# Second layer's cross attention: the negated row maxima as three bf16 parts, added to the scores by a bf16 product

## The chip, the cores and the metric

The kernel runs on one core of one Trainium2 chip. The metric is the device time of one execution, in microseconds, as the median of several runs. The engines named below are PE (TensorE, matmuls; PEld are its weight loads), DVE (VectorE), ACT (ScalarE), POOL (GpSimd) and SP (SyncE, which only starts transfers here).

## The reference

A decoder of two layers on `x`, 16 batch elements of 128 tokens with 128 features, with a context of 77 rows for each batch element. Each layer is attention, cross attention to the context and a feed forward part, each added to its input and normalised. The first layer's feed forward is a mixture of experts. What the change touches is the second layer's cross attention, with 16 heads of 8 features:

```python
q = (einsum('bse,fe->bsf', query, wq) + bq).reshape(B, Sq, H, D).transpose(0, 2, 1, 3)
k = (einsum('bse,fe->bsf', key, wk) + bk).reshape(B, Sk, H, D).transpose(0, 2, 1, 3)
v = (einsum('bse,fe->bsf', value, wv) + bv).reshape(B, Sk, H, D).transpose(0, 2, 1, 3)
scores = einsum('bhqd,bhkd->bhqk', q, k) * scale
attn = softmax(scores, axis=-1)          # over the 77 context rows
out = einsum('bhqk,bhkd->bhqd', attn, v) # then the output projection
```

The softmax subtracts the maximum over the 77 keys for each query and head before the exponential. It is this subtraction that is done in another way.

## The kernel before

The work has three stages. In the first (to about 400 us) the first layer's attention and cross attention run over the 16 batch elements. In the second the experts run. The third, from about 458 us, holds the whole second layer, and the change belongs to it.

The third stage is software pipelined. `ORDER2` is a table that gives each engine the order of its steps within one round; the number behind a colon shifts a step by so many batch elements. In one round the decay attention (steps `d_...`) works on the next batch element, the cross attention (`e_...`) on the present one, and the feed forward part (`f_...`) on both sides of it. Each engine runs its list in order, and semaphores make it wait for the others. A step that waits holds all that stands behind it on its engine.

The cross attention of one batch element, with 16 heads as 4 strips of 32 partitions (index `i`) times 4 (index `a`):

- `e_s` (PE): scores with queries on the partitions, four banks of 4 x 77 columns.
- `e_m0` to `e_m3` (DVE, `row_max`, L1347): the negated maxima of a bank, 4 columns of the tile `nmb`.
- `e_nm` (PE, L942; ACT, L1095): `nmb` is turned by a transpose against the fp32 identity `ident` and copied to `nmT`, so that heads lie on partitions.
- `e_st` (PE, the rows `bank<-qa,k`): the scores again, now with keys on the partitions, 16 products that are left open.
- `e_inj` (PE, `less_max`, the rows `bank<-nmT,k_sb`): 16 products of a selecting table `picksel` with `nmT` add the negated maxima to the open scores. Each takes one strip of 32 partitions.
- `e_e0` to `e_e3` (ACT, L1105): the exponentials, then `e_v` (PE) with values and sums.

Around them on PE stand `f_up` (the convolution as products, `bank<-k,xdT`) ahead of `e_nm`; then `d_s01` (the first decay scores, `bank<-kbd`, weights `kbd`), `e_st`, `d_s3`, `e_inj` and `d_v` (`bank<-k,va`). On DVE `e_m3` is followed by `d_k` (L1657, which makes the keys that `d_s01` multiplies and which waits for POOL's `d_fade`), then `d_m0` and `d_m1` (the causal masks, L1663), `f_clamp` (L1755), `d_m2`, `d_m3` and `f_silu` (L1728). `d_s01` waits for `d_k`, `d_m0` for `d_s01`, `d_s3` for `d_m0`, `d_v` for `d_m3`. On ACT the order is `e_nm`, `f_exp`, `f_sig` (two passes, L1210 and L1211), then `e_e0`.

In the expert stage DVE runs, between relus of the experts' hidden rows (`m_hid`, L1578) and copies (`m_y`), `bias_parts`: it already splits the convolution's bias into three bf16 parts (L1612 to L1615).

Of the kernel before, what the change touches and what calls it, by code (L numbers as in the profile page):

```python
# [14 lines left out]
P = 128  # L15
B = 16
# [35 lines left out]
def offsets(sizes):  # L52
    at, found = 0, {}
    for name, n in sizes.items():
# [93 lines left out]
            "d_gate:2 d_q:2 e_m0:1 e_m1:1 e_m2:1 e_m3:1 d_k:2 d_m0:2 d_m1:2").split(),  # L148
    "act": ("e_e2 d_v:1 e_e3 c_ln:2 d_ln:1 e_v d_x:2 d_ln2:1 f_turn:-1 e_ln e_x:1 d_gates:2 e_q:1 f_ln:-1 f_x "
# [28 lines left out]
def decoder(nc, x_in, xT_in, cT_in, w_a, w_k, w_b, w_l, w_f, w_up, w_down, columns, rows, conv, consts, out,  # L178
            rel_dram, xg_dram, yg_dram):
    with ExitStack() as ctx:  # L180
        def sb(name, shape, dt=F32):
            return ctx.enter_context(nc.sbuf_tensor(name, shape, dt))
# [42 lines left out]
        ident = const("ident")  # L225
        picksel = const("picksel").rearrange("p (a j) -> p a j", a=4)

# [18 lines left out]
        nmxb, sumb, recb = sb("nmxb", [P, H]), sb("sumb", [P, H]), sb("recb", [P, H])  # L246
        nmb = sb("nmb", [P, P])
        nmT = sb("nmT", [P, P])
        rba = sb("rba", [P, P])
# [66 lines left out]
        ve, vd = va[0:2], va[2]  # L316
        nme, nmTe = nmb, nmT
        xE, xD = x1[0:2], [pTa[:, 6 + i, :] for i in range(2)]
# [138 lines left out]
        def _(pool):  # L457
# [3 lines left out]
            for t in va:  # L461
                G.memset(t[:], 0.0).then_inc(pre_pool, 1)
            G.memset(nmb[:], 0.0).then_inc(pre_pool, 1)
            G.memset(cum[:, 0, :], 0.0).then_inc(pre_pool, 1)
# [93 lines left out]
        def _(pe):  # L558
# [151 lines left out]
            def less_max(ps, ready):  # L710

                for a in range(4):
                    for i in range(4):
                        last = mm(ps[i][0:C, a * P:(a + 1) * P], picksel[strip(i), a, :], nmT[strip(i), :],
                                  start=False, stop=(a == 3))
                        if a == 3:
                            last.then_inc(ready, 1)
# [222 lines left out]
            def e_nm(t):  # L940
                pe.wait_ge(maxed["b"], 4 * (B + t) + 4)
                pe.transpose(bank[6][:, 3 * P:4 * P], nme[:], ident).then_inc(nm_ps, 1)  # L942

# [296 lines left out]
        def _(dve):  # L1240
# [103 lines left out]
            def row_max(i, b, base=0):  # L1344
                def f(t):
                    dve.wait_ge(scores["b"], 4 * (base + t) + i + 1)
                    V.tensor_reduce(nmb[:, 32 * i:32 * i + 4], bank[b][:, 0:4 * C].rearrange("p (a j) -> p a j", a=4),  # L1347
                                    AX.X, ALU.max, negate=True).then_inc(maxed["b"], 1)
                return f

            def b_max(i):
# [255 lines left out]
            def bias_parts():  # L1607

                dve.wait_ge(ld_conv, 32)
                step(V.tensor_scalar(cbias, cbias, const("third", 0, 1)[0:32, :], None, ALU.mult))  # L1610
                for i in (1, 2):
                    step(V.tensor_copy(cpart, cbias))  # L1612
                    step(V.scalar_tensor_tensor(out=cbias, in0=cpart, scalar=const("third", i, i + 1)[0:32, :], in1=cbias,
                                                op0=ALU.mult, op1=ALU.add))
                V.tensor_copy(cbrow[0:32, :], cbias).then_inc(w_ready, 1)  # L1615

# [147 lines left out]
            for n in range(1, 2 * E, 2):  # L1764
# [23 lines left out]
                **{f"d_m{i}": d_mask(i) for i in range(4)}, "d_add": d_out, "d_n0": d_n0, "d_n1": d_n1, "d_norm": d_norm,  # L1788
                **{f"e_m{i}": row_max(i, 3 + i, B) for i in range(4)}, "e_div": divide("e", 3, rbe, oTe), "e_add": e_out,
                "e_norm": norm("e", lambda t: xE[t % 2][:], normed["e"]), "v1": v1,  # L1790
# [5 lines left out]
def tables():  # L1796
    p, t = np.arange(P)[:, None], np.arange(P)[None, :]
    h2 = DH // 2
    freq = (1.0 / 10000.0 ** (np.arange(h2, dtype=np.float32) / np.float32(h2))).astype(np.float32)
    angle = (np.arange(P, dtype=np.float32)[None, :] * freq[(np.arange(P) % DH) // 2][:, None]).astype(np.float32)  # L1800
    sign = np.where(p % 2 == 0, -1.0, 1.0)
    n = np.arange(E + 1)
    row = np.arange(2 * B)
    band = np.arange(160)
    parts = {
        "ident": p == t,
        "tri": p < t,
        "causal": p <= t,
        "cos": np.cos(angle), "sin": np.sin(angle) * sign,
        "time": np.broadcast_to(t - MID, (P, P)),  # L1810
        "head16": (p // R) % 2 == np.arange(2),
        "rev": np.broadcast_to(E + 1 - n, (P, E + 1)),
        "cap": np.broadcast_to(np.where(n < E, CAP, 0), (P, E + 1)),
        "base": np.broadcast_to(n * P, (P, E + 1)),
        "trash": SLOTS + row[None, :] * P + p,
        "picksel": np.repeat(p % 32 == np.arange(4), C, axis=1),
        "onesband": np.broadcast_to(band % 40 < DH, (P, 160)),
        "third": np.concatenate([p < 3, -1 * (p >= 1), -1 * (p == 2)], axis=1),
    }
    return np.concatenate([np.asarray(parts[k], np.float32) for k in CONSTS], axis=1)  # L1820
# [81 lines left out]
```

## Time and profile before

| | |
|---|---|
| median of 3 runs | 760.44 us (759.88 to 760.55) |
| the profiled execution | 758.19 us |
| its span in the profile | 756.4 us |
| PE busy | 675.0 us, 89% of the span |
| DVE busy | 551.8 us, 73% |
| ACT busy | 404.5 us, 53% |
| POOL busy | 207.3 us, 27% |

The span is what the profiler sees from the first to the last instruction; the execution's own time is 1.8 us longer. Busy shares are means over three stages with different limits. An fp32 product appears as two records of a matmul, a bf16 product or a transpose as one. A weight load (PEld) can run while an earlier product is still under way.

### The profile page before, as it was taken

To read this page: it belongs to the slowest core of one execution; us is meant where nothing else is said; L and a number is where in the kernel's file an instruction comes from. 1 tells how busy PE (TensorE), PEld (TensorE's weight loads), DVE (VectorE), ACT (ScalarE), POOL (GpSimd) and SP (SyncE) were. 2 spreads that over 40 slices of the span, in tenths; PEclk is the share of its full clock that TensorE was granted. 3 is DMA by queue.
4 is the path that set the end of the run, shared out by engine and by line. 5 is a ranking of instruction groups with operands and counts; after the bars stand their busy time and mean duration, and the time that the engine had idled before them with its cause. 6 is when DMAs were issued, how large, how long until landed. Compare 5 with 4: busy or idle time off the path is not lost.

```text
span 756.4 us, 21349 instructions
## 1 busy us (share of the span) xinstructions
PE 675.0 (89%) x8334; PEld 519.1 (69%) x8334; DVE 551.8 (73%) x2013; ACT 404.5 (53%) x1172; POOL 207.3 (27%) x213
## 2 busy tenths in 40 slices
PE   5888999999999999999878988899899989999886
PEld 2445777777777787777766976666666666666664
DVE  1236778888888888987647557888888788888853
ACT  3756666666766666663210224555555555555542
POOL 5312233333333315423344112222222222222100
PEclk9969999999999999999879999999999999999999
DMA  9776435555444455630032110000000011111000
GB/s 345 271 257 205 162 130 172 171 171 170 166 160 124 123 172 178 231 147 20 20 103 69 33 32 9 10 11 13 13 16 13 13 14 14 15 13 13 5 6 7
DMA packets 48259, 72.22 MB, mean 95 GB/s; under 512 B 2832, under 2 KB 43280, under 8 KB 45472
## 3 DMA queue, kind: packets, MB, share of 16 engines
q1 hardware_dynamic: 45120, 61.80, 24.3%
q0 software_dynamic: 2320, 5.18, 3.3%
q10 hardware_dynamic: 720, 3.88, 1.3%
q8 instruction: 67, 1.10, 0.6%
q14 instruction: 32, 0.26, 0.1%
HBM read 32.38 MB, written 38.47 MB: 94 GB/s over the span
## 4 chain that ended last, share of the span: by engine, by line
PE 58%; DVE 22%; issue 8%; ACT 7%; DMA 2%; another core or an unknown queue 1%; POOL 1%; SPq 0%; DVEq 0%; ACTq 0%
PE bank L560 49%; PE bank L621 4%; PE bank L706 3%; DVE k L1663 3%; DVE scol L1705 2%; ACT kbd L1210 1%; ACT kbd L1211 1%; DMA xT_ld<-xT 1%; DVE k L1641 1%; DVE kbd L1755 1%; DVE q L1732 1%; DVE y_d L1679 1%; ACT pTb L1105 1%; DVE stats_e L1313 1%
## 5 line engine op out<-in xcount | busy, mean ns | idle before, releaser
L1066 ACT ACTIVATE sc<-sc,nmxa 128x128 f32<-128x128 f32 x256 | 79.9, 393 | 34.9 <-DVE nmxa L1290 34.9
L499 POOL TENSOR_TENSOR early<-early,recb 128x616 f32<-128x616 f32 x32 | 38.9, 1216 | 187.6 <-DVE recb L1378 187.6
L1290 DVE CUSTOM_DVE_ANT_0 sc<-bank,rel 128x128 f32<-128x128 f32 x256 | 56.4, 286 | 14.7 <-PE bank L560 14.5
L1663 DVE TENSOR_TENSOR k<-bank,k_sb 128x512 f32<-128x512 f32 x64 | 41.2, 685 | 28.6 <-PE bank L560 23.7
L1300 DVE COPY pTa<-bank 128x512 f32<-128x512 f32 x32 | 22.0, 690 | 32.7 <-PE bank L621 32.7
L1046 ACT ACTIVATE rext<-bank 128x512 f32<-128x512 f32 x64 | 34.8, 609 | 18.2 <-PE bank L560 18.2
L476 POOL TENSOR_TENSOR rext<-rext,ones 128x1008 f32<-128x1008 f32 x16 | 29.9, 1868 | 52.7 <-ACT rext L1046 52.7
L560 PE MATMUL bank<-k,xdT 128*128 128x512 f32 x96 | 43.8, 592 | 0.0
L535 POOL TENSOR_TENSOR oTb<-x_all,row_sb 128x128 f32<-128x128 f32 x16 | 7.3, 457 | 132.9 <-DVE pTa L1684 132.9
L1113 ACT ACTIVATE early<-early 128x308 f32<-128x308 f32 x64 | 27.4, 454 | 29.4 <-DVE early L1363 29.4
L621 PE MATMUL bank<-k_sb,sc 128*128 128x128 f32 x256 | 36.4, 288 | 7.3 <-issue 6.5
L560 PE MATMUL bank<-pTb,v 77*32 77x128 f32 x1024 | 34.5, 282 | 4.4 <-issue 2.2
L560 PEld LDWEIGHTS bank<-xTb,wb 128*128 128x128 f32 x256 | 29.8, 191 | 12.6 <-issue 12.6
L621 PEld LDWEIGHTS bank<-k_sb,sc 128*128 128x128 f32 x256 | 30.2, 148 | 11.9 <-issue 11.0
L508 POOL DMA_INDIRECT xg_dram<-x_all,to_slot x32 | 31.4, 980 | 24.8 <-DVE to_slot L1514 16.8
L525 POOL DMA_INDIRECT pTa<-yg_dram,of_slot x32 | 31.3, 980 | 23.3 <-DMA yg_dram<-sc 16.3
L1354 DVE TENSOR_REDUCE nmxb<-bank 128x4 f32<-128x308 f32 x64 | 28.8, 472 | 11.6 <-PE bank L560 8.1
L560 PE MATMUL bank<-kbd 32*128 32x256 f32 x256 | 36.2, 400 | 0.1
L560 PE MATMUL bank<-k_sb,ones 128*128 128x256 f32 x144 | 36.2, 401 | 0.0
L1105 ACT ACTIVATE pTb<-bank 77x512 f32<-77x512 f32 x64 | 34.2, 588 | 3.4 <-PE bank L560 3.4
L560 PE MATMUL bank<-wb,oTb 128*128 128x128 f32 x256 | 34.6, 292 | 1.0 <-issue 0.6
L706 PE MATMUL bank<-k_sb,early 128*77 128x128 f32 x256 | 33.4, 274 | 0.8 <-ACT xTb L1095 0.5
(275 smaller groups left out, 1839.3 us busy)
## 6 DMA issues: line engine op xcount, KB each, us to landing
rel_dram<-rext SPq DMA_DIRECT2D x16, 2040.0 KB, 7.3
rel<-rel_dram SPq DMA_DIRECT2D x16, 960.0 KB
rext<-w_up SPq DMA_DIRECT2D x1, 1792.0 KB, 9.4
rel<-w_down SPq DMA_DIRECT2D x1, 1792.0 KB, 7.7
wb<-w_b ACTq DMA_DIRECT2D x1, 1604.0 KB, 16.5
xT_ld<-xT SPq DMA_DIRECT2D x16, 64.0 KB, 7.3
x_all<-x ACTq DMA_DIRECT2D x1, 1024.0 KB, 11.8
rel<-rel_dram SPq DMA_DIRECT2D x16, 64.0 KB
```

The costliest lines, as they stand in the source:

```text
L476: G.tensor_tensor(rext[:, :, 0:MAX_REL - 1], rext[:, :, MAX_REL - 1:MAX_REL].broadcast_to(shape), ones[:, 0:1].unsqueeze(2).broadcast_to(s ...
L499: G.tensor_tensor(pB[:, part, :], pB[:, part, :], recb[:, part].unsqueeze(2).broadcast_to([P, 8, C]), ALU.mult).then_inc(b_even, 1)
L508: G.indirect_dma_start(out=xg_dram, out_offset=bass.IndirectOffsetOnAxis(ap=to_slot[:, 2 * t + k:2 * t + k + 1], axis=0), in_=x_all[:, t, ...
L525: G.indirect_dma_start(out=g[k][t % 3], out_offset=None, in_=yg_dram if t else yg_dram[0:(E + 1) * P], in_offset=bass.IndirectOffsetOnAxis ...
L560: return pe.matmul(out_, lhsT, rhs, start=start, stop=stop)
L621: last = pe.transpose(bank[i][:, a * P:(a + 1) * P], sc[:, 4 * i + a, :], ident)
L706: last = pe.transpose(bank[(6, 7, 4, 5)[i]][0:C, a * P:(a + 1) * P], pB[:, 4 * i + a, :], ident)
L1046: A.activation(rext[:, 4 * i:4 * i + 4, MAX_REL - 1:MAX_REL - 1 + P], bank[i][:].rearrange("p (a r) -> p a r", a=4), ACT.Copy).then_inc(r_ ...
L1066: last = A.activation(sc[:, h, :], sc[:, h, :], ACT.Exp, bias=nmxa[:, h:h + 1], scale=-1.0)
L1105: A.activation(dst[0:C, 4 * i:4 * i + 4, :], bank[b][0:C, :].rearrange("p (a i) -> p a i", a=4), ACT.Exp).then_inc(exped["b"], 1)
L1290: last = V.tensor_tensor_reduce(out=sc[:, h, :], in0=bank[i][:, a * P:(a + 1) * P], in1=rel[:, t % 2, h, :], scale=-1.0, scalar=FAR, op0=A ...
L1663: V.tensor_tensor(scd[:, 4 * i:4 * i + 4, :], bank[(1, 2, 0, 1)[i]][:].rearrange("p (a t) -> p a t", a=4), const("causal").unsqueeze(1).br ...
```

## The change

The four maxima of a strip no longer go straight into the tile that is turned, but into a small dense tile `nmx` (128 x 16, fp32). A new DVE step `e_sp` (`e_split`) behind `e_m3` splits them into three bf16 numbers that add up to the fp32 one: the value rounded to bf16, the remainder rounded to bf16, and what is then left. The three parts stand in 12 columns of each strip of `nme`, now a bf16 tile. `e_nm` turns it by an ordinary product with a bf16 identity, ACT copies it to the bf16 tile `nmTe`, and the injection multiplies it by a bf16 table in which each head picks all three of its parts. The two bf16 tables are cast once on DVE, in `bias_parts`. PE now waits for one count of `e_sp` in place of four of the maxima.

```diff
-            "d_gate:2 d_q:2 e_m0:1 e_m1:1 e_m2:1 e_m3:1 d_k:2 d_m0:2 d_m1:2").split(),
+            "d_gate:2 d_q:2 e_m0:1 e_m1:1 e_m2:1 e_m3:1 e_sp:1 d_k:2 d_m0:2 d_m1:2").split(),
...
-        nmb = sb("nmb", [P, P])
-        nmT = sb("nmT", [P, P])
+        nmx = sb("nmx", [P, 16])
+        nmr = sb("nmr", [P, 16])
+        nme = sb("nme", [P, P], BF16)
+        nmTe = sb("nmTe", [P, P], BF16)
+        identb = sb("identb", [P, P], BF16)
+        pickb = sb("pickb", [P, 4 * C], BF16)
...
-                        last = mm(ps[i][0:C, a * P:(a + 1) * P], picksel[strip(i), a, :], nmT[strip(i), :],
+                        last = mm(ps[i][0:C, a * P:(a + 1) * P], pickb[strip(i), a * C:(a + 1) * C], nmTe[strip(i), :],
                                   start=False, stop=(a == 3))
...
             def e_nm(t):
-                pe.wait_ge(maxed["b"], 4 * (B + t) + 4)
-                pe.transpose(bank[6][:, 3 * P:4 * P], nme[:], ident).then_inc(nm_ps, 1)
+                pe.wait_ge(maxed["b"], 4 * B + t + 1)
+                mm(bank[6][:, 3 * P:4 * P], nme[:], identb[:]).then_inc(nm_ps, 1)
...
-                    V.tensor_reduce(nmb[:, 32 * i:32 * i + 4], bank[b][:, 0:4 * C].rearrange("p (a j) -> p a j", a=4),
-                                    AX.X, ALU.max, negate=True).then_inc(maxed["b"], 1)
-                return f
+                    keep(f"e_m{i}", t, V.tensor_reduce(
+                        nmx[:, 4 * i:4 * i + 4], bank[b][:, 0:4 * C].rearrange("p (a j) -> p a j", a=4),
+                        AX.X, ALU.max, negate=True))
+                return f
+
+            def e_split(t):
+                by_strip = nmx[:].rearrange("p (i a) -> p i a", a=4)
+                left = nmr[:].rearrange("p (i a) -> p i a", a=4)
+                parts = [nme[:].rearrange("p (i x) -> p i x", x=32)[:, :, 4 * k:4 * k + 4] for k in range(3)]
+                after(max(done[f"e_m{i}", t] for i in range(4)))
+                need(dve, nm_ps, t)
+                step(V.tensor_copy(parts[0], by_strip))
+                V.tensor_tensor(left, by_strip, parts[0], ALU.subtract)
+                step(V.tensor_tensor(parts[1], by_strip, parts[0], ALU.subtract))
+                V.tensor_tensor(parts[2], left, parts[1], ALU.subtract).then_inc(maxed["b"], 1)
...
+                step(V.tensor_copy(identb[:], ident))
+                step(V.tensor_copy(pickb[:], const("picksel")))
                 V.tensor_copy(cbrow[0:32, :], cbias).then_inc(w_ready, 1)
...
-        "picksel": np.repeat(p % 32 == np.arange(4), C, axis=1),
+        "picksel": np.repeat((p % 32 < 12) & (p % 4 == np.arange(4)), C, axis=1),
```

`step(...)` makes DVE wait until the instruction has completed; an instruction without it lets the next one start behind it.

DVE's order in a round of the third stage, before. `out_sb` belongs to `f_norm`, the first `kbd` to `d_q`, `nmb` to the maxima, the second `kbd` to `d_k`, `k<-bank` to the masks.

```order
L1332 TENSOR_SCALAR out_sb<-y_f,mv_f,rstd_f 128x128 [waits f_inv,st_out0]
L1751 TENSOR_SCALAR k<-k 128x256 [waits d_gate0]
L1651 TENSOR_TENSOR kbd<-bank,early 128x512 [waits d_rank]
L1347 TENSOR_REDUCE nmb<-bank 128x4 [waits b_scores] x4
L1657 TENSOR_TENSOR kbd<-bank,k 128x256 [waits d_faded,d_rank]
L1663 TENSOR_TENSOR k<-bank,k_sb 128x512 [waits d_att] x2
```

The same place after:

```order
L1667 TENSOR_TENSOR kbd<-bank,early 128x512 [waits d_rank]
L1349 TENSOR_REDUCE nmx<-bank 128x4 [waits b_scores] x4
L1360 CAST nme<-nmx 128x4x4 [waits nm_ps,dve_step]
L1361 TENSOR_TENSOR nmr<-nmx,nme 128x16 [waits dve_step]
L1362 TENSOR_TENSOR nme<-nmx,nme 128x4x4
L1363 TENSOR_TENSOR nme<-nmr,nme 128x4x4 [waits dve_step]
L1673 TENSOR_TENSOR kbd<-bank,k 128x256 [waits d_faded,d_rank]
L1679 TENSOR_TENSOR k<-bank,k_sb 128x512 [waits d_att] x2
```

Four instructions have come between the maxima and `d_k`; three of them wait for one before (`dve_step`).

PE's order from the convolution to the decay values, before. `kbd` are the weights of `d_s01` and `d_s3`, `qa,k` is `e_st`, `nmT,k_sb` the injection, `k,va` is `d_v`.

```order
L560 MATMUL bank<-k,xdT 128x512 x3
L942 MATMUL bank<-k_sb,nmb 128x128 [waits b_maxed]
L560 MATMUL bank<-kbd 128x256 [waits d_v,d_qkd]
L560 MATMUL bank<-kbd 128x256 x5
L560 MATMUL bank<-qa,k 77x128 [waits nm_sb]
L560 MATMUL bank<-qa,k 77x128 x15
L560 MATMUL bank<-kbd 128x256 [waits d_masked]
L560 MATMUL bank<-nmT,k_sb 77x128 x16
L560 MATMUL bank<-k,va 32x128 [waits d_masked]
```

And after:

```order
L562 MATMUL bank<-k,xdT 128x512 x3
L562 MATMUL bank<-identb,nme 128x128 [waits b_maxed]
L562 MATMUL bank<-kbd 128x256 [waits d_v,d_qkd]
L562 MATMUL bank<-qa,k 77x128 [waits nm_sb]
L562 MATMUL bank<-nmTe,pickb 77x128 x16
L562 MATMUL bank<-k,va 32x128 [waits d_masked]
```

On PE nothing has moved; the turn and the injection have other operands.

DVE in the expert stage, after. `cbrow` is the convolution's bias, `oTb<-bank` the next relu; before, the first two rows are not there.

```order
L1629 CAST identb<-k_sb 128x128 [waits dve_step]
L1630 CAST pickb<-k_sb 128x308 [waits dve_step]
L1631 CAST cbrow<-k 32x512 [waits dve_step]
L1592 TENSOR_SCALAR oTb<-bank 128x512 [waits m_down,m_up]
```

The two casts stand ahead of a relu that PE needs.

## Rows read from the trace of the kernel before

**Rows 1.** The page, chain of waits: share of the span by engine.

```profile
PE 58%; DVE 22%; issue 8%; ACT 7%; DMA 2%; another core or an unknown queue 1%; POOL 1%; SPq 0%; DVEq 0%; ACTq 0%
```

**Rows 2.** Table by windows: stretch, its length, busy us of each engine, clock, DMA.

```profile
core 0: us, PE busy (x) PEld busy (x) DVE busy (x) ACT busy (x) POOL busy (x), PEclk, DMA share, GB/s
656.00:674.00 18.00, 16.30 (x240) 12.08 (x233) 14.91 (x50) 10.21 (x31) 4.01 (x6) 1.00 0.14 13
```

**Rows 3.** Chain in order of time, one round: start, us, what.

```profile
601.03 3.63 PE bank L560 x15
604.66 0.11 PE bank L942
604.77 1.11 PE bank L560 x11
605.88 1.27 DVE k L1663 x2
```

**Rows 4.** Timeline, steady round: start, us, engine, instruction, count, idle before and releaser.

```profile
602.15 1.62 DVE L1347 TENSOR_REDUCE nmb<-bank 128x4 f32<-128x308 f32 x4
603.69 0.42 DVE L1657 TENSOR_TENSOR kbd<-bank,k 128x256 f32<-128x256 f32 x1
604.07 0.14 PEld L942 LDWEIGHTS bank<-k_sb,nmb 128*128 128x128 f32 x1 [0.24 <-DVE nmb L1347]
604.49 0.27 PE L942 MATMUL bank<-k_sb,nmb 128*128 128x128 f32 x1
604.69 0.74 PEld L560 LDWEIGHTS bank<-kbd 32*128 32x128 f32 x12 [0.49 <-issue]
605.86 1.29 DVE L1663 TENSOR_TENSOR k<-bank,k_sb 128x512 f32<-128x512 f32 x2 [1.75 <-PE bank L560]
607.57 1.03 PE L560 MATMUL bank<-nmT,k_sb 32*77 32x128 f32 x20
608.72 1.54 ACT L1105 ACTIVATE pTb<-bank 77x512 f32<-77x512 f32 x3
608.73 0.81 PEld L560 LDWEIGHTS bank<-k,va 128*32 128x32 f32 x32 [0.36 <-DVE k L1663]
```

**Rows 5.** Timeline, routing on DVE: small operations, the second unwaited by the third.

```profile
396.14 0.17 DVE L1462 TENSOR_TENSOR one_hot<-one_hot,hit 128x16 f32<-128x16 f32 x1
396.35 0.17 DVE L1463 TENSOR_TENSOR picked<-one_hot 128x8 f32<-128x8 f32 x1
396.43 0.17 DVE L1490 TENSOR_TENSOR r_ok<-bank,k_sb 128x16 f32<-128x16 f32 x1
```

**Rows 6.** Timeline, `d_k` and the load of `d_s01` in rounds 0, 1 and 6.

```profile
460.32 0.42 DVE L1657 TENSOR_TENSOR kbd<-bank,k 128x256 f32<-128x256 f32 x1
460.79 0.74 PEld L560 LDWEIGHTS bank<-kbd 32*128 32x128 f32 x12 [0.18 <-DVE kbd L1657]
...
476.74 0.41 DVE L1657 TENSOR_TENSOR kbd<-bank,k 128x256 f32<-128x256 f32 x1
478.11 0.74 PEld L560 LDWEIGHTS bank<-kbd 32*128 32x128 f32 x12 [0.49 <-issue]
...
568.19 0.42 DVE L1657 TENSOR_TENSOR kbd<-bank,k 128x256 f32<-128x256 f32 x1
568.83 0.74 PEld L560 LDWEIGHTS bank<-kbd 32*128 32x128 f32 x12 [0.36 <-DVE kbd L1657]
```

**Rows 7.** Timeline, PE in round 15: the turn.

```profile
730.24 0.27 PE L942 MATMUL bank<-k_sb,nmb 128*128 128x128 f32 x1
```

**Rows 8.** Timeline, expert stage: DVE's small work, the relu behind it, PE's loads.

```profile
428.54 0.29 DVE L1605 TENSOR_SCALAR early<-early 128x256 f32<-128x256 f32 x1
433.89 0.67 DVE L1578 TENSOR_SCALAR oTb<-bank 128x512 f32<-128x512 f32 x1
434.56 0.97 PEld L560 LDWEIGHTS bank<-rel,oTb 128*128 128x128 f32 x8
437.65 0.14 PEld L862 LDWEIGHTS bank<-k_sb,x_all 128*128 128x128 f32 x1 [0.33 <-DVE x_all L1332]
```

**Rows 9.** Table by windows and timeline: PE ahead of round 0, and in a steady round.

```profile
451.00:456.00 5.00, 3.77 (x17) 3.26 (x18) 3.10 (x12) 1.73 (x8) 0.67 (x2) 0.66 0.00 0
...
453.49 2.07 PE L560 MATMUL bank<-oTa,wl 128*128 128x128 f32 x8
615.19 1.06 PE L560 MATMUL bank<-oTa,wl 128*128 128x128 f32 x8
```

More of the change, by code:

```diff
@@ L225, in decoder @@
         ident = const("ident")
-        picksel = const("picksel").rearrange("p (a j) -> p a j", a=4)
         x_all = sb("x_all", [P, B, P])
@@ L316, in decoder @@
         ve, vd = va[0:2], va[2]
-        nme, nmTe = nmb, nmT
         xE, xD = x1[0:2], [pTa[:, 6 + i, :] for i in range(2)]
@@ L462, in _ @@
                 G.memset(t[:], 0.0).then_inc(pre_pool, 1)
-            G.memset(nmb[:], 0.0).then_inc(pre_pool, 1)
+            G.memset(nme[:], 0.0).then_inc(pre_pool, 1)
             G.memset(cum[:, 0, :], 0.0).then_inc(pre_pool, 1)
@@ L1788, in _ @@
                 **{f"d_m{i}": d_mask(i) for i in range(4)}, "d_add": d_out, "d_n0": d_n0, "d_n1": d_n1, "d_norm": d_norm,
-                **{f"e_m{i}": row_max(i, 3 + i, B) for i in range(4)}, "e_div": divide("e", 3, rbe, oTe), "e_add": e_out,
+                **{f"e_m{i}": row_max(i, 3 + i, B) for i in range(4)}, "e_sp": e_split, "e_div": divide("e", 3, rbe, oTe), "e_add": e_out,
                 "e_norm": norm("e", lambda t: xE[t % 2][:], normed["e"]), "v1": v1,
```

## The prediction

> **What bounds the kernel now.** I read the profile from coarse to fine. The page's chain of waits [rows 1] puts 58% of the span on PE and 22% on DVE, so a saving on PE looks welcome; but that share is a mean over three stages. The change acts only in the last one (458 us to the end), which runs in rounds, one batch element of each of its three parts per round. The table by windows [rows 2] shows such a round: of 18.00 us PE is busy 16.30, DVE 14.91, ACT 10.21, at full clock. No engine is full, so what counts is the order in which they wait. The chain in order of time [rows 3] shows where the changed step stands in a round: PE runs the convolution (`f_up`), the turn of the maxima (`e_nm`, L942) and the first decay scores (`d_s01`, "PE bank L560 x11"), and then hands over to DVE's masks (L1663). From there the chain stays on DVE and ACT until the next round's PE stretch. The injection itself (`e_inj`) is not in that chain.
>
> The timeline of one round [rows 4] gives the reason, to 0.01 us. The reader should see five things.
> 1. The fourth row maximum ends at 602.15 + 1.62 = 603.77. `d_k` (L1657) follows, 603.69 to 604.11.
> 2. PE loads the maxima at 604.07, 0.30 after they are ready, because it is still in `f_up`. The turn itself starts at 604.49 and the next weights (`d_s01`) at 604.69. So the turn holds PE for 0.20.
> 3. `d_s01` needs `d_k`, done at 604.11, and starts at 604.69. Where PE really waits for `d_k`, the load starts 0.05 after its end: in round 0, 460.32 + 0.42 = 460.74, then 460.79 [rows 6]. So `d_k` has 604.69 - 604.16 = 0.53 us to spare in the steady round.
> 4. DVE then idles 1.75 until the scores are there (605.86). Work added on DVE before `d_k` is inside this gap, and yet only 0.53 of it is free.
> 5. The injection ends near 608.60 (607.57 + 1.03). What comes after it on PE (`d_v`) starts at 608.73, released by DVE's last mask, with the weight load idle 0.36. The exponentials that need the injection start at 608.72, where ACT comes from its sigmoids. Both consumers are there later than the injection.
>
> **What the change removes.** The injection is 16 fp32 products, 32 records of a matmul in the trace, and becomes 16 bf16 ones. The last 20 records take 1.03 [rows 4]; the whole may be shorter by 0.5 to 1 us a round. By point 5 that is worth nothing: `d_v` still waits for DVE, and the exponentials for ACT. PE only waits longer at `d_v`. If DVE and ACT were early there, the same saving would count in full; that is a rival below. The turn becomes a bf16 product of 128 columns. It held PE 0.20 and may hold it 0.05 (a quarter, my estimate from the halves into which the trace splits fp32 products); that is a gain of up to 0.15 a round, but only where PE does not wait for `d_k` anyway. The copy on ACT keeps its shape and I price its difference at nothing.
>
> **What it adds in a round.** Four small DVE operations of 16 elements a partition stand between the fourth maximum and `d_k`, three of them behind a wait for their forerunner. No row of before shows this very form; the nearest are the routing operations [rows 5], also 16 elements. One takes 0.17. Start to start it is 0.21 where the next one waits for it (396.14 to 396.35) and 0.08 where it does not (396.35 to 396.43). So: the cast starts at 603.77 + 0.03 = 603.80; the first subtraction 604.00; the second, unwaited, 604.08; the third 604.29, ending 604.46; `d_k` starts 0.08 after it, at 604.37. Against 603.69 that is **0.68 later**. The weights of the turn can be loaded at 604.51 instead of 604.07, the product follows at once, and it must only be through by the time `d_s01` may start. `d_k` ends at 604.79, `d_s01`'s weights start at 604.84 instead of 604.69: **0.15 us a round**. Queued behind the wait on PE are `d_s01`, then `e_st`, `d_s3` and the injection; DVE's masks wait for `d_s01`, `f_clamp` stands behind the masks in DVE's order, ACT's sigmoids wait for `f_clamp`. So the 0.15 goes down the whole chain. Bounds for the 0.68: if all four cost only 0.08, it is 0.35 and PE starts `d_s01` 0.15 earlier than now (the shorter turn); if each costs 0.21 plus 0.03, it is 0.96 and the delay 0.43. I take 0.68, since it is put together from both kinds of spacing as the code has them.
>
> The Trainium skill bears on this at one place. Rows 5 show a Vector operation starting 0.08 after the one before, whose own duration is 0.17. The page VectorE: DVE Perf Modes, section The DRAIN you can't avoid, says that the next operation does not start until the pipe is empty and that leaving out semaphores saves nothing. By that rule all four and `d_k` would be spaced 0.21, the shift would be about 0.9 and the delay 0.4 a round, some 3 us more in all. The trace disagrees for neighbours without a wait, and the sum goes by the trace.
>
> **Other rounds.** The spare differs, and rows 6 give it from the same two instructions.
> - Round 0 (460 us): PE already waits for the maxima and for `d_k`. No spare, so the whole 0.68.
> - Round 1 (478 us): `d_k` ends at 476.74 + 0.41 = 477.15 and `d_s01` loads at 478.11. Spare 0.91; the shorter turn can show: -0.15.
> - Rounds 2 and 3: as in the steady round, spare about 0.6: 0.08 each, 0.16 together.
> - Round 6 (568 us): `d_k` ends at 568.61, loads at 568.83. Spare 0.17, so 0.51.
> - The other ten, 4 to 14 without 6: 0.15 each, 1.5.
> - Round 15: no decay part, DVE has time. The turn starts at 730.24 behind `f_up` [rows 7] and is a little shorter: -0.05.
> Together 0.68 - 0.15 + 0.16 + 0.51 + 1.5 - 0.05 = 2.65.
>
> **What it adds once.** Two casts (128 and 308 elements) go into the expert stage, ahead of a relu (`m_hid`). SBUF to SBUF, 256 elements take 0.29 [rows 8]; over the 0.17 of the smallest operations [rows 5] that is 0.12 for 256, so the two come to 0.23 and 0.31, with 0.03 behind each 0.60. The relu starts at 433.89, straight behind the cast there, and runs 0.67, to 434.56; PE's next load is at 434.56 too, so there is no slack. What may swallow part of it is the 0.33 that PE waits for `x_all` at 437.65. Bounds 0 and 0.60, taken 0.4. The memset only changes its tile.
>
> **Sum.** 2.65 + 0.4 = **+3.05 us**. The profiled execution took 758.19 (span 756.4 and 1.8 around it), so it would take 761.2. The median of the runs shown is 760.44, 2.3 above that execution; the difference holds for both: **763.5**.
>
> **Rivals.**
> - *The split fits into the spare.* The four operations cost 0.53 or less. Speaks for it: the bound of 0.35. Against: the 0.21 in rows 5, which recurs in the whole routing code. Left are round 0 with about 0.5 and the casts with 0.4, less 0.15 in round 1: 761.2, no measurable change. Chance 0.16.
> - *PE is what holds `d_v` and the exponentials, and the bf16 injection shortens the chain* (the other side). It decides if DVE's last mask is done before the injection ends. Then 14 rounds save up to 0.5 each, -7, against +3: 756.4. Against: the load of `d_v` idles 0.36 in front of DVE's mask in the steady rounds [rows 4]. Chance 0.06.
> - *DVE is the bound and pays for all of it.* 0.68 in each of 15 rounds is 10.2, with the casts 10.6: 771. For: DVE's long run in the chain. Against: its idle 1.75 just behind the added work. A milder form is slower subtractions on strided bf16 (delay 0.43 a round, 15 rounds, 6.5 and the casts 0.4): 767. Chance for both 0.12.
> - *PE's clock.* PE gets more idle time: behind the injection, and in round 0, where it already waits. At 451 to 456 us the granted clock was 0.66 and 8 records took 2.07 instead of 1.06 [rows 9], after waits for ACT and DVE. That is its lower level, 1.2 GHz, in part of the stretch. If round 0's longer wait or the steady wait brings that about, I price it at 1.5 to 3 us: 766. Against: the granted clock is 1.00 in a steady round with all its waits [rows 2]. Chance 0.06.
> - The forecast: 0.60.
>
> **How the numbers follow.** About 0.2% (1.5 us) is what this kernel's times can tell from no change. Faster is the second rival, with a little of the first: 0.07. The first rival and the low end of the forecast are within 0.2%: 0.17. Slower: 0.76. The forecast's own range is 762.0 to 765.5. For 8 in 10 the low end takes in the rival that hides the split, and the high end the slower subtractions in half: 760.6 to 766.5.
>
> **What would show it.** In the changed trace, four DVE operations between the maxima and `d_k`, spaced about 0.2, 0.08, 0.2, 0.08; `d_s01`'s weight load 0.05 behind `d_k` in rounds 2 to 14, with DVE named as releaser; DVE's idle before the masks down from 1.75 to about 1.2; the idle before `d_v` up from 0.36 to about 0.9 (the injection shorter, the mask no earlier); a period of the steady round longer by 0.15. If `d_s01` starts where it did, the split was hidden; if `d_v` starts earlier relative to the masks, I misjudged who holds it.

## The result and the profile after

| | before | after |
|---|---|---|
| median of 4 runs | 760.16 us (758.17 to 760.55) | 795.95 us (792.03 to 797.63) |
| the profiled execution | 758.19 us | 794.73 us |
| its span | 756.4 us | 792.9 us |
| mean granted clock of PE | 0.971 | 0.913 |
| PE busy | 675.0 us | 708.4 us |

The changed kernel is slower by a ratio of 1.0469 [1.0424, 1.0515]. The forecast was 763.5 us, with a range up to 766.5: wrong by 32 us. Six more runs, taken later, gave 1.0407 [1.0354, 1.046] (`y1_after_again` below). The ratios are the recorded ones, from the single runs, and can differ by some tenths of a per cent from the quotient of two medians.

The page shows where to look first. These are its granted clock in 40 slices (tenths of full speed) and the chain by engine, of the changed kernel:

```profile
span 792.9 us, 20918 instructions
PE 708.4 (89%) x8078; PEld 551.5 (70%) x8078; DVE 564.6 (71%) x2079; ACT 405.2 (51%) x1172; POOL 206.9 (26%) x213
PEclk9978999999999999999799988888888888888889
PE 62%; DVE 19%; ACT 9%; issue 6%; DMA 1%; another core or an unknown queue 1%; POOL 1%; SPq 0%; DVEq 0%; ACTq 0%
```

The same clock row of the kernel before is

```profile
PEclk9969999999999999999879999999999999999999
```

From slice 24 on (456 us) the clock reads 8 where it read 9, in all of the second layer, and PE's share of the chain went from 58% [rows 1] to 62%. PE is busy 33 us longer, although it has 256 records of matmuls fewer.

The place is found with the table by windows. This is one round of the changed kernel cut at its waits; columns as in [rows 2]:

```profile
604.00:608.00 4.00, 3.64 (x66) 2.78 (x65) 2.78 (x7) 1.43 (x4) 1.49 (x3) 1.00 0.22 37
608.00:610.00 2.00, 1.08 (x32) 0.81 (x32) 1.84 (x4) 2.00 (x5) 0.00 (x0) 1.00 0.00 0
610.00:611.00 1.00, 0.73 (x10) 0.55 (x14) 0.93 (x6) 0.70 (x3) 0.00 (x0) 0.98 0.00 0
611.00:617.00 6.00, 6.00 (x78) 5.62 (x69) 3.92 (x17) 2.73 (x10) 0.86 (x2) 0.50 0.01 4
618.00:624.00 6.00, 5.64 (x36) 3.65 (x36) 5.50 (x20) 2.94 (x10) 1.15 (x2) 1.00 0.04 11
```

And the kernel before over two of these stretches, which hold nearly the same steps there:

```profile
608.00:610.00 2.00, 1.69 (x47) 1.18 (x39) 1.84 (x4) 1.97 (x5) 0.00 (x0) 1.00 0.04 8
611.00:617.00 6.00, 5.10 (x91) 4.50 (x92) 5.27 (x24) 3.24 (x13) 0.87 (x2) 1.00 0.01 3
```

Up to 611 us the clock is full. Then it is at its lower level, 0.50 or 1.2 GHz, and PE never rests in the next six microseconds (6.00 busy of 6.00, where it was 5.10 before). What preceded the fall is the stretch 608 to 610: PE busy 1.08 of 2.00, where it was 1.69. In short windows the low stretch lasts 6.8 us. It comes back in each of rounds 1 to 14, at 488, 508, 529, 549 us and so on to 754 us, and for 3.4 us in round 0. With one of 3.4 us ahead of the rounds, at 453 us, and one at the very end, where PE has no work left, that is 17 falls from 450 us on and 103.4 us at the lower level. Before, it was two falls, at 452 us ahead of the rounds and at 753 us behind PE's last product, and 6.8 us.

The timeline of the same round has the instructions. First DVE in the changed kernel, against [rows 4] and [rows 5]:

```profile
603.42 0.17 DVE L1360 CAST nme<-nmx 128x16 bf16<-128x16 f32 x1
603.62 0.18 DVE L1361 TENSOR_TENSOR nmr<-nmx,nme 128x16 f32<-128x16 f32 x1
603.72 0.17 DVE L1362 TENSOR_TENSOR nme<-nmx,nme 128x16 bf16<-128x16 f32 x1
603.92 0.17 DVE L1363 TENSOR_TENSOR nme<-nmr,nme 128x16 bf16<-128x16 f32 x1
604.01 0.42 DVE L1673 TENSOR_TENSOR kbd<-bank,k 128x256 f32<-128x256 f32 x1
605.65 1.29 DVE L1679 TENSOR_TENSOR k<-bank,k_sb 128x512 f32<-128x512 f32 x2 [1.22 <-issue]
```

Then PE and ACT of the changed kernel, where the brackets give the idle time before and its releaser:

```profile
604.15 0.10 PEld L562 LDWEIGHTS bank<-identb,nme 128*128 128x128 bf16 x1 [0.71 <-DVE nme L1363]
604.48 0.74 PEld L562 LDWEIGHTS bank<-kbd 32*128 32x128 f32 x12 [0.24 <-DVE kbd L1673]
607.15 0.59 PE L562 MATMUL bank<-nmTe,pickb 32*77 32x128 bf16 x7
608.51 1.54 ACT L1107 ACTIVATE pTb<-bank 77x512 f32<-77x512 f32 x3
608.52 0.81 PEld L562 LDWEIGHTS bank<-k,va 128*32 128x32 f32 x32 [0.94 <-DVE k L1679]
608.52 1.08 PE L562 MATMUL bank<-k,va 128*32 128x128 f32 x32 [0.78 <-DVE k L1679]
610.27 0.49 PE L562 MATMUL bank<-wl,xTr 128*128 128x128 f32 x2 [0.66 <-ACT xTr L1097]
610.75 1.78 PE L562 MATMUL bank<-pTb,va 77*32 77x128 f32 x32
612.28 1.96 PE L562 MATMUL bank<-pTb,k_sb 77*32 77x128 f32 x32
616.15 1.85 PE L562 MATMUL bank<-oTa,wl 128*128 128x128 f32 x8
```

In the kernel before, the two sets of `e_v`, 32 records each, are:

```profile
610.96 1.08 PE L560 MATMUL bank<-pTb,va 77*32 77x128 f32 x32
611.86 1.06 PE L560 MATMUL bank<-pTb,k_sb 77*32 77x128 f32 x32
```

The reader should see three things. The waits are just those foretold: the four operations 0.20, 0.10, 0.20, 0.09 apart, `d_s01` released by `d_k`, the load of `d_v` idle 0.94 instead of 0.36. `d_v` itself runs at the old speed. But two steps later `e_v` takes 1.78 and 1.96 instead of 1.08 and 1.06, and the eight records of `oTa,wl` take 1.85 instead of 1.06 [rows 9]: everything that stands on PE in those 6.8 us takes nearly twice as long.

The sum closes. From the first maximum of round 0 to that of round 15 the kernel before needs 268.75 us (its steady rounds take 17.93, but two that take 18.65), the changed one 303.83 (eleven rounds in a row at 20.47 or 20.48). Those 35.1 us are nearly all of the 36.5 by which the spans differ.

### The profile page after: what moved, and what is told of

It is laid out like the page before. It is cut to its first block, busy times and chain, and to the rows that moved or that the text cites. A ratio compares the mean times of both kernels' runs of the same rounds, so it can differ in the third digit from the quotient of the medians.

```text
span 792.9 us, 20918 instructions
## 1 busy us (share of the span) xinstructions
PE 708.4 (89%) x8078; PEld 551.5 (70%) x8078; DVE 564.6 (71%) x2079; ACT 405.2 (51%) x1172; POOL 206.9 (26%) x213
## 3 DMA queue, kind: packets, MB, share of 16 engines
q8 instruction: 65, 1.06, 0.5%
## 4 chain that ended last, share of the span: by engine, by line
PE 62%; DVE 19%; ACT 9%; issue 6%; DMA 1%; another core or an unknown queue 1%; POOL 1%; SPq 0%; DVEq 0%; ACTq 0%
PE bank L562 51%; PE bank L623 4%; PE bank L708 3%; DVE nmx L1349 3%; ACT pTb L1107 3%; DVE k L1679 3%; PE bank L990 2%; ACT kbd L1212 1%; ACT kbd L1213 1%; ACT sc L1068 1%; PE bank L864 1%; DVE x L1334 1%; DVE kbd L1771 1%; DVE k L1657 1%
## 5 line engine op out<-in xcount | busy, mean ns | idle before, releaser
L1292 DVE CUSTOM_DVE_ANT_0 sc<-bank,rel 128x128 f32<-128x128 f32 x256 | 56.4, 286 | 13.7 <-PE bank L562 13.4
L562 PE MATMUL bank<-oTa,wl 128*128 128x128 f32 x192 | 37.0, 356 | 0.0
L562 PEld LDWEIGHTS bank<-oTa,wl 128*128 128x128 f32 x192 | 35.9, 275 | 0.3 <-ACT oTa L1097 0.3
```

The source lines that it names most:

```text
L562: return pe.matmul(out_, lhsT, rhs, start=start, stop=stop)
L1292: last = V.tensor_tensor_reduce(out=sc[:, h, :], in0=bank[i][:, a * P:(a + 1) * P], in1=rel[:, t % 2, h, :], scale=-1.0, scalar=FAR, op0=A ...
```

## The experiments

There are twelve kernels. "Falls" are those of the profiled execution from 450 us to its end; in each of them the last one lies behind PE's last product and costs nothing. "Period" is that of its steady rounds. Each ratio is to the kernel before on the same chip. Four theories are weighed: A, the shorter injection leaves PE too little to do and its clock falls; B, products in bf16 are slow here; C, it is the split's wait; and within A, that all of PE's waits count or only the one at `d_v`.

| run | median us | ratio [95%] | us at lower level (falls) | period |
|---|---|---|---|---|
| x1_fill8 | 755.86 | 1.0046 [1.001, 1.0081] | 13.7 (3) | 18.08 |
| x2_fp32_split | 754.45 | 1.0043 [1.0007, 1.008] | 1.9 (1) | 18.08 |
| x3_one_part | 773.61 | 1.0283 [1.0252, 1.0314] | 72.9 (12) | 20.12 to 20.44, or 17.87 to 17.93 |
| x4_before_short | 777.79 | 1.0314 [1.0282, 1.0345] | 80.9 (13) | 19.80 to 20.68, or 17.92 to 18.29 |
| y1_after_again | 791.95 | 1.0407 [1.0354, 1.046] | 103.6 (15) | 20.47 |
| y2_fill_up | 794.38 | 1.0473 [1.0432, 1.0515] | 107.6 (16) | 20.47 |
| x3_one_part_fill8 | 755.75 | 0.9965 [0.9941, 0.999] | 2.0 (1) | 17.87 |
| y3_turn_bf16 | 757.18 | 0.9993 [0.9971, 1.0015] | 9.2 (3) | 17.87 |
| z1_fill_in_dv | 759.10 | 1.0109 [1.0065, 1.0152] | 1.3 (1) | 18.22 |
| z2_fill4 | 753.98 | 1.0039 [1.0001, 1.0077] | 1.1 (1) | 18.10 |
| z3_before_fill8 | 755.77 | 1.0047 [1.0025, 1.0069] | 1.0 (1) | 18.02 |
| z4_before_casts | 752.45 | 1.0005 [0.998, 1.0031] | 9.2 (3) | 17.92 |

The kernel before itself had a median of 751.92 beside the first four, 758.52 beside the next four and 752.54 beside the last four.

### x1_fill8: the changed kernel, with PE kept at work

```diff
+                for n in range(8):
+                    i, a = n % 4, n // 4 % 4
+                    mm(bank[3 + i][0:C, a * P:(a + 1) * P], zf[strip(i), 0:C], zf[strip(i), :], start=False, stop=False)
                 less_max(bank[3:7], turned)
```

`zf` is a tile of fp32 zeros, set once by POOL, so that the eight products add nothing to the open scores.

> The changed kernel with 8 fp32 products of zeros (about 0.06 us each, together 0.5) ahead of the injection, on the same strips and banks. They add nothing to the scores; they only keep PE busy as long as the fp32 injection did. Theory A (the clock: the shorter injection leaves PE idle before d_v, and PE falls to its lower level later in each round): the idle before d_v goes from 0.94 back to about 0.4, the mean granted clock from 0.91 back to 0.97, and the time to 763 to 766 us. Theory B (bf16 products on strips, or the switch between bf16 and fp32, are slow in themselves): no change or slower, 796 to 803. Theory C (the wait for the split in front of e_nm is what drops the clock): the clock stays at 0.91 and the time at 795.

Of 17 falls three are left, only one of them in a round (the first, which takes 19.92), and of the loss 0.5%. The page's clock row and the load of `d_v` in this kernel:

```profile
PEclk9969999999999999999999998999999999999999
609.49 0.81 PEld L564 LDWEIGHTS bank<-k,va 128*32 128x32 f32 x32 [0.50 <-DVE k L1684]
```

The bf16 turn, the bf16 injection and the split are all still there. So neither B nor C is what costs 35 us; with 16 more records on PE in each round the kernel is 4% faster. `d_v`'s load still waits for DVE's mask, and the filler has merely taken the place of idle time.

### x2_fp32_split: the split alone, all in fp32

```diff
-        nme = sb("nme", [P, P], BF16)
-        nmTe = sb("nmTe", [P, P], BF16)
-        identb = sb("identb", [P, P], BF16)
-        pickb = sb("pickb", [P, 4 * C], BF16)
+        nme = sb("nme", [P, P])
+        nmTe = sb("nmTe", [P, P])
+        identb = sb("identb", [P, P])
+        pickb = sb("pickb", [P, 4 * C])
...
-                mm(bank[6][:, 3 * P:4 * P], nme[:], identb[:]).then_inc(nm_ps, 1)
+                pe.transpose(bank[6][:, 3 * P:4 * P], nme[:], ident).then_inc(nm_ps, 1)
```

> The changed kernel with its four new tiles in fp32: DVE's four operations and the two copies stay, but the turn is the fp32 transpose again and the injection 16 fp32 products. Theory A (clock, by the shorter injection): clock 0.97, and the time is that of before plus what the split costs on DVE, forecast as 3.2: 762 to 765 us. Theory B (bf16 products slow): also 762 to 765. Theory C (the wait for the split drops the clock): 790 or more, clock about 0.91.

This is the price of the split by itself: a period of 18.08 against 17.93, so the 0.15 a round that was forecast, and a first round of 17.14 against 16.42, 0.7 where 0.68 was forecast. From round 0 to 15 it is 271.0 against 268.75, +2.25. The ratio of 1.0043 would be 763.4 us on the 760.16 of the first comparison. DVE and PE in a steady round of this kernel:

```profile
598.71 0.42 DVE L1673 TENSOR_TENSOR kbd<-bank,k 128x256 f32<-128x256 f32 x1
599.18 0.74 PEld L562 LDWEIGHTS bank<-kbd 32*128 32x128 f32 x12 [0.19 <-DVE kbd L1673]
600.34 1.29 DVE L1679 TENSOR_TENSOR k<-bank,k_sb 128x512 f32<-128x512 f32 x2 [1.22 <-PE bank L562]
603.21 0.81 PEld L562 LDWEIGHTS bank<-k,va 128*32 128x32 f32 x32 [0.36 <-DVE k L1679]
```

`d_s01` loads 0.05 behind the end of `d_k`, as foretold, and `d_v`'s idle is back at the 0.36 of [rows 4]. The same wait, with the long injection, leaves the clock alone: C falls.

### x3_one_part: bf16 throughout, and no split

```diff
-                    keep(f"e_m{i}", t, V.tensor_reduce(
-                        nmx[:, 4 * i:4 * i + 4], bank[b][:, 0:4 * C].rearrange("p (a j) -> p a j", a=4),
-                        AX.X, ALU.max, negate=True))
+                    V.tensor_reduce(nme[:, 32 * i:32 * i + 4], bank[b][:, 0:4 * C].rearrange("p (a j) -> p a j", a=4),
+                                    AX.X, ALU.max, negate=True).then_inc(maxed["b"], 1)
...
-        "picksel": np.repeat((p % 32 < 12) & (p % 4 == np.arange(4)), C, axis=1),
+        "picksel": np.repeat(p % 32 == np.arange(4), C, axis=1),
```

The step `e_sp` goes, and PE waits for the four maxima as in the kernel before.

> The changed kernel without the split: the maxima are written straight as one bf16 number (the remainder is left out; a softmax may subtract any number near its maximum), turned and injected in bf16. DVE's order is that of before. Theory A: the injection is as short as in the changed kernel, so the clock falls all the same, 0.91 to 0.92; 787 to 794 us, that is the changed kernel's time less the 3 of the split. Theory C: clock 0.97 and 757 to 760. Theory B: as theory A in the time, so this run tells C from the others.

Slower by 2.8% without any split. Two stretches of this kernel, one that escapes and one that does not:

```profile
590.00:610.00 20.00, 17.66 (x226) 12.10 (x224) 16.48 (x54) 10.17 (x31) 5.71 (x8) 1.00 0.06 12
610.00:630.00 20.00, 18.21 (x218) 13.99 (x217) 15.68 (x50) 10.22 (x31) 3.98 (x6) 0.83 0.10 11
```

Here ten rounds have a full fall and take 20.12 to 20.44, and the others take 17.87 to 17.93. That is less than theory A had foretold (a clock of 0.91 to 0.92 and the changed kernel's time less the split's 3 us; the clock was 0.934), since it had reckoned with a fall in every round. What sets the falling rounds apart is not the length of PE's waits. These are PE's two waits ahead of the place, in two rounds in a row:

```profile
596.14 1.08 PE L562 MATMUL bank<-k,va 128*32 128x128 f32 x32 [0.78 <-DVE k L1667]
597.88 0.49 PE L562 MATMUL bank<-wl,xTr 128*128 128x128 f32 x2 [0.66 <-ACT xTr L1097]
614.00 1.08 PE L562 MATMUL bank<-k,va 128*32 128x128 f32 x32 [0.78 <-DVE k L1667]
615.74 0.64 PE L562 MATMUL bank<-wl,xTr 128*128 128x128 f32 x2 [0.66 <-ACT xTr L1097]
```

The waits are the same to 0.01 us, and the clock stays up at 598 us and falls at 616 us. So the shorter injection makes falls possible, and something else, that no run here isolates, decides in which rounds they come.

### x4_before_short: the kernel before, with less injection

```diff
-                for a in range(4):
+                for a in (3,):
                     for i in range(4):
```

> The kernel before, all in fp32, with 12 of the injection's 16 products left out (the maxima of 12 heads are not subtracted). The injection is about 0.75 us shorter, as with bf16, and there is no bf16 product and no split. Theory A: PE idles before d_v as in the changed kernel, the clock falls to 0.91 to 0.92, and a kernel with less work takes 785 to 795 us. Theories B and C: 760 or a little less, clock 0.97.

This is the plainest of the twelve. Nothing is in bf16 here, nothing is split, and twelve fp32 products a round are simply not made: the kernel does less and is 3.1% slower. That is again somewhat less than foretold, with eleven rounds that fall and a clock of 0.924. Two lines of one round, then the table by windows for a low stretch and for one without a fall:

```profile
619.88 0.81 PEld L560 LDWEIGHTS bank<-k,va 128*32 128x32 f32 x32 [1.01 <-DVE k L1663]
622.10 1.78 PE L560 MATMUL bank<-pTb,va 77*32 77x128 f32 x32
624.00:628.00 4.00, 4.00 (x44) 3.62 (x37) 2.71 (x11) 2.10 (x8) 0.64 (x2) 0.50 0.02 4
630.00:650.00 20.00, 17.30 (x225) 12.79 (x222) 16.92 (x60) 11.42 (x36) 4.00 (x6) 1.00 0.09 11
```

The same signature as in the changed kernel: `e_v` at 1.78, the clock at 0.50, PE without a pause. Theory B is done with.

### y1_after_again: the changed kernel once more

> The changed kernel once more, beside the next three on the same chip, so that their clocks and times can be compared. 1.04 to 1.05 of before, mean clock 0.91, the clock at its lower level for a part of every steady round.

The time at the lower level is that of the first trace, 103.6 us for 103.4. Rounds 2 to 14 have a fall of 6.8 us each; in rounds 0 and 1 there is a single one, which lasts 13.7 us from 461.8 us on. Of the six runs five lie between 789.22 and 792.59; one took 782.59 with a mean clock of 0.929 instead of 0.913 to 0.917, so that now and then some rounds of this kernel escape as well.

### y2_fill_up: filling in front of the turn

```diff
+                mm(bank[7][:, 0:P], zf[:], zf[:], start=False, stop=False)
```

It stands in the sum of `f_up`, behind the bias row.

> The changed kernel with one fp32 product of zeros (0.21 us) added to the convolution's sum, so that PE waits less for the split in front of e_nm; the idle before d_v stays. Theory A1 (both idle times count together; the injection's alone drops the clock in fewer rounds, as in the one-part kernel and in the kernel before with the short injection, 10 or 11 rounds): fewer rounds at the lower level than the changed kernel, clock 0.93, ratio 1.03 to 1.035. Theory A2 (only the idle before d_v counts): as the changed kernel, 1.045. Rival (any extra idle is harmless, PE has more to do and so is slower): 1.05.

It did nothing for the clock: 107.6 us at the lower level, one long fall over rounds 0 and 1 and one in each of rounds 2 to 14 as in y1_after_again, and a period of 20.47. The turn with its load and the products of `d_v` in this kernel:

```profile
603.91 0.10 PEld L564 LDWEIGHTS bank<-identb,nme 128*128 128x128 bf16 x1 [0.48 <-DVE nme L1366]
604.09 0.22 PE L564 MATMUL bank<-identb,nme 128*128 128x128 bf16 x1
608.28 1.08 PE L564 MATMUL bank<-k,va 128*32 128x128 f32 x32 [0.78 <-DVE k L1682]
```

The idle of the load in front of the turn shrank from 0.71 to 0.48, that before `d_v` stayed, and the clock fell at `e_v` as before. So A1 of the expectation is wrong: a round's waits are not equally good to fill. 0.23 us here did nothing, and about as much right ahead of `d_v` is enough (z2_fill4).

### x3_one_part_fill8: one part, and filler

> The one-part kernel (bf16 turn and injection, no split on DVE, remainder left out) with 8 fp32 products of zeros ahead of the injection. Theory A: the clock is back at 0.97, and since DVE's order is that of before and the turn holds PE 0.15 us less a round, the time is 0.997 of before (0.9955 to 1.0). If the clock falls in any round, 1.01 or more: then 8 products are not enough, or the shorter turn matters too.

The edits are those of x3_one_part and of x1_fill8 together. It is the one version that comes out faster than both kernels, by 0.35%, with an interval that just leaves out 1. Its turn and `d_v` in a steady round:

```profile
598.67 0.10 PEld L564 LDWEIGHTS bank<-identb,nme 128*128 128x128 bf16 x1 [0.24 <-DVE nme L1354]
599.10 0.22 PE L564 MATMUL bank<-identb,nme 128*128 128x128 bf16 x1
599.24 0.74 PEld L564 LDWEIGHTS bank<-kbd 32*128 32x128 f32 x12 [0.48 <-DVE kbd L1666]
603.28 0.81 PEld L564 LDWEIGHTS bank<-k,va 128*32 128x32 f32 x32 [0.50 <-DVE k L1672]
```

From the turn's start to the next weights it is 0.14, where it was 0.20 [rows 4]; the period is 17.87 against 17.93. Over the rounds this makes some 0.8 us, 0.1%; where the rest of the 0.35% would come from is not shown. One bf16 part is enough for the softmax, since whatever is subtracted is the same for all 77 keys of a query and head, and cancels when the exponentials are divided by their sum; the rounded maximum only has to keep them in range.

### y3_turn_bf16: only the turn in bf16

```diff
-        nmTe = sb("nmTe", [P, P], BF16)
+        nmTe = sb("nmTe", [P, P])
...
-                        last = mm(ps[i][0:C, a * P:(a + 1) * P], pickb[strip(i), a * C:(a + 1) * C], nmTe[strip(i), :],
+                        last = mm(ps[i][0:C, a * P:(a + 1) * P], const("picksel")[strip(i), a * C:(a + 1) * C], nmTe[strip(i), :],
```

Otherwise it is x3_one_part, without the second cast.

> One bf16 part of the maxima (remainder left out, no split), turned by a bf16 product, but copied out as fp32 and injected by the fp32 products of before. Only the turn is shorter. Theory A: clock as before, 0.997 (0.9955 to 1.0). It would beat both kernels by what the turn saves, if that 0.15 us a round is on the chain. If the turn's saving is no gain, 1.000.

The period is 17.87 again, so it is the turn that gives 0.06 a round. Over 14 rounds that is 0.8 us, 0.1%, and the median cannot tell it from nothing. The injection is in fp32, and the falls are as few as in z4_before_casts, whose turn and injection are those of the kernel before (3 each).

### z1_fill_in_dv: filling behind the wait for the mask

```diff
+                        if a in (1, 2):
+                            mm(bank[2][strip(s), 0:P], zf[:, 0:32], zf[:], start=False, stop=False)
```

The eight products stand between those of `d_v`, so PE waits for the mask as long as in the changed kernel.

> The changed kernel with 8 fp32 products of zeros (0.4 us) among d_v's own products, so behind the long idle of PE and not in it: the idle before d_v stays 0.94, the one after d_v shrinks. Theory A (PE's idle time around d_v counts as a sum, wherever it is filled): no or few falls of the clock, 1.005 to 1.01. Theory A2 (only the idle in front of d_v counts): falls as in the changed kernel, 1.04 to 1.05.

One fall, and no more: the theory that the wait at `d_v` alone brings the clock down is refuted. In this kernel the wait is as long as ever, and it is the next one that is shorter:

```profile
605.90 0.41 PEld L564 LDWEIGHTS bank<-k,va 128*32 128x32 f32 x16 [0.93 <-DVE k L1683]
606.36 0.44 PE L564 MATMUL bank<-zf 128*32 128x128 f32 x8
607.84 0.49 PE L564 MATMUL bank<-wl,xTr 128*128 128x128 f32 x2 [0.37 <-ACT xTr L1101]
```

PE idles 0.37 before `wl,xTr` where it was 0.66. As in x1_fill8 a little more work close ahead of the fall is enough, on either side of that wait. Here it is also in the chain: the period is 18.22, the longest of the cured kernels. Its 1.0109 rests on four runs, and its interval overlaps that of x1_fill8.

### z2_fill4, z3_before_fill8: how little is enough, and what filler costs

z2_fill4 has `range(4)` in place of `range(8)`. z3_before_fill8 has the filler of x1_fill8 in the kernel before.

> The changed kernel with 4 products of zeros ahead of the injection in place of 8 (0.25 us of the 0.6 that the bf16 injection saves). Theory A says only that fewer rounds fall or none: 1.004 with clock 0.97 if 4 are enough, 1.03 to 1.045 if not. It tells how near the kernel before stood to the fall.

> The kernel before with the 8 products of zeros ahead of its own fp32 injection: what such a filling costs where the clock does not need it. The injection ends 0.5 us later, at about the time of d_v's start and the first exponential: 0.1 to 0.5 us a round, 1.002 to 1.008. If it gains (under 0.998), the gain of the one-part kernel with filling is the filling's and not the turn's.

Four products, eight records, do as well as eight: no fall in any round, 1.0039. They shorten the idle of `d_v`'s load from 0.94 to 0.72, by 0.22 a round. A fp32 zero product of one strip takes about 0.06, since eight of them shorten `d_v`'s idle from 0.94 to 0.50. In the kernel before, the filler is no cure for anything and costs 0.09 a round (18.02 against 17.93). Its ratio of 1.0047 [1.0025, 1.0069] is more than these 1.3 us over 14 rounds; the rest was not traced. So the kernel before stood near the edge without showing it: x4_before_short gave it less to do by twelve products of about 0.06, 0.7 us a round, and fell; the changed kernel saved 0.65 (its injection runs from 606.41 to 607.74, 1.33, where it ran from 606.62 to 608.60, 1.98), and fell in every round; with 0.22 of that given back it falls in none.

### z4_before_casts: the two casts alone

```diff
+                step(V.tensor_copy(identb[:], ident))
+                step(V.tensor_copy(pickb[:], const("picksel")))
                 V.tensor_copy(cbrow[0:32, :], cbias).then_inc(w_ready, 1)
```

> The kernel before with only the two casts added in the expert stage (their results are not used). Forecast 0.4 us: 1.0005 (1.000 to 1.001). Rival: hidden, 1.000. Any change above 1.002 means that the stage before the rounds moves more than I said.

1.0005 [0.998, 1.0031]: the 0.4 us are within what this measurement can resolve, and so is nothing at all. The term is neither shown nor refuted.

## Why the prediction was wrong

**The step that failed is point 5 and what was made of it: "By point 5 that is worth nothing", and "PE only waits longer at `d_v`".** That a saving behind a later wait is worth nothing was right as to the chain, and wrong as to the engine: the wait was not free. With PE's longer idle its clock fell in every round, and the low clock stayed on for 6.8 us over work that is on the path. With the clock kept up a round takes 18.08 (x1_fill8, x2_fp32_split); it took 20.47. So the fall costs 2.39 a round. From round 0 to 15 it is 303.83 against the 271.0 of x2_fp32_split: 32.8 us of the 36.5 are the clock's, 2.25 are the split's, and 1.4 lie outside these rounds.

**The mechanism was on the list, with 0.06 and 1.5 to 3 us.** The rival on PE's clock named "round 0's longer wait or the steady wait" and was priced as if it came about once. Two things in it failed. It was sized by a single fall, though a cause that is in every steady round returns in every steady round; and the evidence against it, a granted clock of 1.00 in a steady round [rows 2], says on which side of the edge the kernel stands and not how far from it. z2_fill4 shows that 0.22 us of PE's idle a round, given back, is enough. What the low clock does to PE's work could have been read before, in the 2.07 against 1.06 of [rows 9]; how long a fall lasts with work at hand could not. By estimate, 6.8 us at half the clock are 3.4 us of work lost; the period grew by 2.39, so the other 1.0 went into time in which PE had been idle.

The Trainium skill has both halves of this, in TensorE: Matmul & The Clock Gate. Its section HAM oscillation — how this bites in real kernels ties swings of the clock to long idle gaps between bursts; the section A second HAM failure mode: psum-queue depth-cycling adds a kernel whose PE idles often and briefly, and swings as well. The traces here agree with the second in that no long idle is needed: ahead of the fall at 611 us PE's longest is 0.78 us. The length of one idle does not decide, since the kernel before has one of 0.83 us ahead of its product at 614.87 us and does not fall.

**The terms of the sum, one by one.**
- *The split's 0.68 and the 0.15 a round*: right. The maxima start at 601.76 in place of 602.15 and `d_k` at 604.01 in place of 603.69, so it is 0.71 later against them. The period grew by 0.15 (x2_fp32_split). The operation without a wait starts 0.10 behind its forerunner, those that wait 0.20, as [rows 5] had it.
- *Round 0*: right, 0.7 for 0.68.
- *Round 1 at -0.15*: not to be read. It takes 18.54 in the kernel before, 18.21 in x2_fp32_split, which has no shorter turn, and 18.23 in z4_before_casts, whose rounds have the code of the kernel before.
- *Round 6 at 0.51*: mostly wrong. In the kernel before, the round that ends there takes 18.32 and the next 17.56, twice 17.94 together, so its lateness is given back at once; with the split (x2_fp32_split) they take 18.08 and 18.09. The place pays 0.15 like its neighbours. In z4_before_casts the two rounds take 17.92 and 17.93, so the lateness itself belongs to the execution that was read and not to the kernel.
- *The shorter turn*: over-rated. It holds PE 0.14 and not 0.05 (x3_one_part_fill8), so it gives 0.06 and not 0.15. A bf16 product of 128 columns with its weights is not a quarter of the fp32 transpose.
- *The two casts*: not to be told from nothing.
- *The injection*: 0.65 shorter, inside the 0.5 to 1 forecast, and `d_v`'s idle at 0.94 for "about 0.9". This term was rightly sized and wrongly valued.

Together the terms are near what x2_fp32_split and x1_fill8 measured: 1.0043 [1.0007, 1.008] and 1.0046, against a forecast of 763.5 / 760.44 = 1.0040. That is closer than the terms deserve: two of them were over-rated with opposite signs, round 6 by 0.36 and the shorter turn by 0.09 in each round where it shows. The ordinary accounting holds within what the runs resolve, and the clock is all the rest. Of the rivals, that PE holds `d_v` is refuted (`d_v` waits for DVE in each trace), and that DVE pays for the whole 0.68 too.

**What stays open.** Why x3_one_part and x4_before_short fall in ten or eleven rounds and the changed kernel in all; the split's wait in front of the turn is the difference between the changed kernel and x3_one_part, and yet shortening it (y2_fill_up) helped nothing. A rival that no run tests is that the moment at which the thin stretch comes counts beside how thin it is: the two rounds of x3_one_part with the same waits speak for it. Which stretch ahead of the fall counts is open too; y2_fill_up speaks against the one in front of the turn, and z1_fill_in_dv shows that the one just behind `d_v`'s start does.

## What to carry to other kernels

When an edit takes work from an engine that already waits, look at what the wait does to the engine itself: on PE, compare the granted clock window by window over a few steady rounds, and count as a real risk any saving that turns PE's work into idle in a stretch where it already pauses. A loss that comes back in each round is priced by the number of rounds. A few products of zeros into an open sum, ahead of the wait, are a cheap test for it (0.09 us a round here) and at times the cure.

## What the runs showed of the hardware

- PE at its lower level stays there for 6.8 us in each of 14 rounds, though it is busy 6.00 of 6.00 us in it. In y1_after_again one low stretch lasts 13.7 us.
- No single idle of PE ahead of the fall at 611 us is longer than 0.78 us; it falls after several short ones. The table by windows up to the fall has, of the kernel before and then of the changed one:

```profile
604.00:611.00 7.00, 6.21 (x121) 4.61 (x121) 5.05 (x10) 4.13 (x9) 1.91 (x3) 1.00 0.27 22
```

```profile
604.00:611.00 7.00, 5.46 (x108) 4.14 (x111) 5.55 (x15) 4.12 (x9) 1.49 (x3) 1.00 0.12 21
```

- Such a sum alone is no rule. The kernel before, a little later in the same round, is less busy than that over as long a stretch and does not fall:

```profile
608.00:615.00 7.00, 5.31 (x121) 4.04 (x114) 6.59 (x23) 4.82 (x15) 0.00 (x0) 1.00 0.01 2
```

- Less work can take longer: twelve products fewer a round cost 3.1% (x4_before_short), and four products of zeros more took 4% off the changed kernel's ratio (z2_fill4).
